# Attention values with the softmax weights stationary: three narrow matmuls per query block and key tile

## The chip, the cores and the metric

The kernel runs on one core of a Trainium2 chip. The metric is the time of one execution in device microseconds, as the median of several runs. The core has a matrix engine (TensorE, PE in the profile, its weight loads PEld), VectorE (DVE), ScalarE (ACT), GpSimd (POOL) and the queue of SyncE (SP), which here issues nearly all DMAs. Matmul results land in PSUM, eight banks of 512 f32 columns in each of 128 partitions.

## What is computed

The program is a layer of a perceiver: cross attention of 512 latent rows on 8192 context rows, then a state-space block, a gated MLP and a mixture of experts. The change lies in the attention:

```
q = (scale * (Q @ Wq + bq)).reshape(bs, q_len, NH, DM)      # 512 rows, NH = 16 heads, DM = 64
k = (K @ Wk + bk).reshape(bs, kv_len, NH, DM)               # 8192 rows
v = (V @ Wv + bv).reshape(bs, kv_len, NH, DM)
qk = jnp.einsum('nlhd,nshd->nhls', q, k)
a = jax.nn.softmax(qk, axis=-1)
o = jnp.einsum('nhls,nshd->nlhd', a, v).reshape(bs, q_len, NH * DM)
return o @ Wo + bo
```

## The kernel before

Products are made from f16 pairs: a number is split into a high part and a low part, and high x high, high x low and low x high are added in PSUM, without low x low.

`context_keys_values` projects the context in 16 chunks of 512 rows, splits keys and values, and stores them in HBM as `kd` and `vd`. In the values tile `vs` each head and key tile has 128 columns: 64 of the high part, 64 of the low part.

`attention` then runs head by head. A key tile has 128 keys, a pair is two of them, so a head has HP = 32 pairs and the stage 512. For a pair:

- TensorE makes the scores transposed, keys on partitions and the 512 queries in columns, with four matmuls of 512 columns (L938, L939) into one of three PSUM buffers `st`.
- ScalarE takes the exponent into `pf`, f32, 128 x 1024 (L771). The high part `ph` is a copy in f16, made by ScalarE for even pairs (L765) and by VectorE for odd ones (L814). VectorE subtracts for the low part `pl` (L818). `pf` has 4 buffers, `ph` and `pl` have 8.
- TensorE adds the values into `acc` (`values`, L890). The value tile is stationary and the softmax weights move, 512 queries wide: for `ph` one matmul per key tile with all 128 columns of `vs` (L900), for `pl` two with 32 columns of the high part each, placed on column groups of the array so that four run at once (L907), and the sum of the weights over the keys by 32 columns of ones, again four at a time (L915). This goes in groups of SP = 4 pairs: the scores of four pairs, then the values of the four pairs before (LAG = 1 group).

At a head's end VectorE copies both banks of `acc` into `parts` (L824, L825). SP stores the sums to HBM and moves the high and low halves onto the partitions of their head in a pair of heads (`store`). For each two heads the sums are read back spread over 128 partitions (`factors`), VectorE adds them and takes the reciprocal (`reciprocals`), SP sends it through HBM so that each partition gets all 512, VectorE scales (`scale`), and ScalarE and VectorE write the split result `oh`, `ol` (`high`, `low`). In the stage's tail TensorE projects with Wo, pair of heads by pair of heads (L957 to L965), VectorE reads the result (L860) and normalizes the rows, and TensorE transposes them (L971).

The order of the work is written out: `turns` and `pair_turns` unroll the steps of one head or two, and the end of a head comes on VectorE two pairs after the head's last pair (`HP + 2`).

Of the kernel before, what the change touches and what calls it, by code (L numbers as in the profile page):

```python
# [21 lines left out]
P = 128  # L22
T = 512
# [67 lines left out]
WT = TW * (NCK // 2 - 1)  # L91

# [166 lines left out]
def context_keys_values(nc, keep, ctxT, q_dram, kd, vd, m_dram, mrow, m_out, wpack, wsplit):  # L259
# [6 lines left out]
    with ExitStack() as ctx:  # L266
# [4 lines left out]
        vs = [m.sb(f"vs{i}", [P, NH, CK // P, 2 * DH], F16) for i in range(2)]  # L271
# [11 lines left out]
        made = m.sem("made")  # L283
# [33 lines left out]
        def _(sp):  # L317
# [12 lines left out]
            def chunk(g, par, i, tiles, more):  # L330
# [6 lines left out]
                at = g * CK if isinstance(g, int) else i * (2 * CK) + (2 - par) * CK  # L337

                for js in (range(0, 6), range(6, 8)) if isinstance(g, int) and g == NCK - 1 else (range(0, 8),):
# [4 lines left out]
                    sp.dma_start(vd.rearrange("h p s -> p h s")[:, :, bass.ds(at + kts.start * P, len(js) // 2 * P)],  # L344
# [9 lines left out]
            for e in range(TW):  # L354
                load_weights(0, e)
            chunk(0, 0, None, (), True)
# [14 lines left out]
        def _(pool):  # L371
            def chunk(g, par, uses, i, tiles):
                nxt = 1 - par
                for n in range(8):
# [11 lines left out]
                    nc.gpsimd.tensor_tensor(vs[par][:, hs, kt, DH:2 * DH],  # L386
# [8 lines left out]

            identity(nc, pool, ident, made)
# [156 lines left out]
SUMS_AT, SCALE_AT, HIGH_AT, LOW_AT, CUT = 8, 14, 16, 18, 20  # L553
EPS1, EPS2 = 1e-5, 1e-6
LAG = 1

HP = KT // 2
SP = 4
HS = HP // SP

# [11 lines left out]
def attention(nc, keep, x, q_dram, m_dram, mrow, m_out, kd, vd, sums, r_dram, bv, bo, n1w, wsplit, xs_dram):  # L572
# [3 lines left out]
    with ExitStack() as ctx:  # L576
# [4 lines left out]
        vs = m.sb("vs", [P, KT, P], F16)  # L581
        ones = m.sb("ones", [P, 32], F16)
        pf = m.sb("pf", [P, FULL, 2, T])
        ph, pl = (m.sb(n, [P, RING, 2, T], F16) for n in ("ph", "pl"))
        parts = m.sb("parts", [P, 2, T])
# [4 lines left out]
        both = [m.sb(n, [P, 2, TT]) for n in ("both_var", "both_sd", "both_rs", "both_tmp")]  # L590
        oh, ol = (keep.big[0][:, i * 2 * WC:(i + 1) * 2 * WC].rearrange("p (j t) -> p j t", t=T) for i in range(2))
        a0, a1, rb, bob = (keep.big[1][:, i * 2 * T:(i + 1) * 2 * T].bitcast(F32) for i in range(4))
        dn = keep.big[1][:, 8 * T:8 * T + 64].bitcast(F32).rearrange("p (n c) -> p n c", c=8)
# [4 lines left out]
        acc = m.ps("acc", [P, 2, T])  # L598
        yp = [st[:, t // 2, t % 2, :] for t in range(TT)]
        hT = [st[:, 2, 0, :], st[:, 2, 1, :], acc[:, 0, :], acc[:, 1, :]]  # L600
# [6 lines left out]
        pl_ready, pv_done, acc_read, o_out = (m.sem(n) for n in ("pl_ready", "pv_done", "acc_read", "o_out"))  # L607
        dn_in, r_ready, r_out, rb_in = m.sem("dn_in"), m.sem("r_ready"), m.sem("r_out"), m.sem("rb_in")
        own_dve, consts, vec_in, small_in = m.sem("own_dve"), m.sem("consts"), m.sem("vec_in"), m.sem("small_in")
        s_ready, oh_ready, ol_ready, y_ready = m.sem("s_ready"), m.sem("oh_ready"), m.sem("ol_ready"), m.sem("y_ready")  # L610
# [10 lines left out]

        FK = SP * 2 * P

# [7 lines left out]
        def _(sp):  # L631
# [7 lines left out]
            def load_values(n, q):  # L639
                sp.dma_start(vs[:, q * 2 * QP:(q + 1) * 2 * QP, :].rearrange("p k c -> p (k c)"),  # L640
                             vd.rearrange("h p s -> p h s")[:, bass.ds(n, 1), q * QK:(q + 1) * QK]
                             .rearrange("p h s -> p (h s)")).then_inc(v_in[q], 16)
# [14 lines left out]
            sp.dma_start(bob, bo.partition_broadcast(P)).then_inc(small_in, 16)  # L657
# [4 lines left out]
            def load_next(h):  # L662
# [5 lines left out]

            def store(j, e):

                h = 2 * j + e
                sp.wait_ge(acc_read, 2 * h + 4)
                sp.dma_start(sums[:, bass.ds(h * T, T)],
                             parts[0:P:32, 1, :]).then_inc(o_out, 16)
                for n, a in enumerate((a0, a1)):
                    sp.dma_start(a[e * DH:(e + 1) * DH, :], parts[n * DH:(n + 1) * DH, 0, :]).then_inc(o_out, 16)

            def factors(j):


                sp.wait_ge(o_out, j * 96 + 144)
# [39 lines left out]
        def turns(eng, step, steps, cut, end=None):  # L721


            for s in range(cut):
                step(0, s)
# [1652 lines left out]
```

## Time and profile before

| | us |
|---|---|
| median of 3 runs | 2517.41 |
| lowest and highest run | 2515.1, 2518.72 |
| span of the profiled execution | 2515.4 |
| TensorE busy | 2395.6 |
| VectorE busy | 1974.4 |
| ScalarE busy | 1603.1 |
| GpSimd busy | 672.5 |

The page gives the span of the profiled execution, from the first to the last instruction; what lies around it is not recorded there. Busy time is the time in which at least one instruction of an engine was running. For TensorE the ends of matmuls are modelled (a 512-column f16 matmul is shown with 0.38 us though the next starts earlier), so the pace of matmuls is read from one start to the next. By stage: projection of keys and values up to 863.8 us, attention from 868.4 to 1789.0 us, its projection and norm to 1822.4 us, then the rest.

### The profile page before, as it was taken

How to read it: one execution, taken by the hardware profiler on the slowest of the kernel's cores; microseconds unless marked ns; L12 is line 12 of the kernel's file. 1: busy time of each engine (PE TensorE's matmuls, PEld its weight loads, DVE VectorE, ACT ScalarE, POOL GpSimd, SP SyncE). 2: the span in 40 equal slices, each digit the busy share in tenths (PEclk: the TensorE clock that was granted, in tenths of full speed). 3: DMA queues.
4: the chain of work that ended last, by engine and by line, in shares of the span. 5: the costliest groups of instructions: out<-in, count | busy, mean ns of one | idle time of the engine just before them, and what ended most of it. 6: DMA issues, size and time to landing. Idle time of an engine off the chain costs nothing. (4 is left out here: it accounts for less than half of the span.)

```text
span 2515.4 us, 39361 instructions
## 1 busy us (share of the span) xinstructions
PE 2395.6 (95%) x14111; PEld 1015.0 (40%) x14111; DVE 1974.4 (78%) x1972; ACT 1603.1 (64%) x1974; POOL 672.5 (27%) x461
## 2 busy tenths in 40 slices
PE   7999999999999799999999999999887878999999
PEld 3333333333333244444444444444332333444554
DVE  5777777777777788888888898888679994267996
ACT  5555555565555478777788777888375442137994
POOL 1455555555555400000000000000019990010001
PEclk9999999999999899999999999999999899999999
DMA  7245654455445593433433333333231005139994
GB/s 251 84 151 163 204 167 150 153 173 175 150 133 150 139 267 89 113 102 95 108 88 105 96 100 92 104 94 107 93 138 52 0 0 201 56 146 346 405 405 174
DMA packets 178205, 366.02 MB, mean 146 GB/s; under 512 B 19545, under 2 KB 90329, under 8 KB 174425
## 3 DMA queue, kind: packets, MB, share of 16 engines
q1 hardware_dynamic: 176610, 360.81, 45.1%
q0 software_dynamic: 1280, 4.20, 0.5%
q8 instruction: 38, 0.62, 0.1%
q14 instruction: 29, 0.24, 0.0%
q10 hardware_dynamic: 248, 0.15, 0.0%
HBM read 254.24 MB, written 106.68 MB: 143 GB/s over the span
## 5 line engine op out<-in xcount | busy, mean ns | idle before, releaser
L466 DVE TENSOR_REDUCE kv_mx<-kv_s 128x1024 f32 (+1 forms) x512 | 595.6, 1218 | 222.5 <-PE kv_s L502 222.5
L818 DVE TENSOR_TENSOR at_pl<-at_pf,at_ph 128x1024 f16<-128x1024 f32 x512 | 613.2, 1223 | 113.2 <-ACT at_ph L765 104.4
L771 ACT ACTIVATE at_pf<-at_st 128x1024 f32<-128x1024 f32 x512 | 497.3, 1025 | 187.2 <-PE at_st L939 182.2
L938 PE MATMUL at_st<-keep_big,at_k_cur 128*128 (+1 forms) x1024 | 390.5, 381 | 10.0 <-DMA keep_big<-q_dram 7.1
L939 PE MATMUL at_st<-keep_big,at_k_one 128*128 (+1 forms) x1024 | 388.9, 380 | 0.0
L765 ACT ACTIVATE at_ph<-at_pf 128x1024 f16<-128x1024 f32 x256 | 272.9, 1066 | 0.0
L1135 POOL MEMSET mamba_zero<- 128x2 f32 x1 | 0.1, 100 | 939.8 <-POOLq L60 939.8
L900 PE MATMUL at_acc<-at_ph,at_vs 128*128 128x512 f16 x1024 | 242.4, 379 | 2.9 <-DVE at_pl L818 2.8
L382 POOL TENSOR_TENSOR kv_ksl<-kv_kf,kv_ksh 128x512 f16<-128x512 f32 x128 | 148.0, 1156 | 246.4 <-ACT kv_ksh L410 246.4
L1049 PE MATMUL kv_kp<-first_ch,first_wkh 128*128 128x512 f16 x512 | 195.0, 381 | 4.2 <-DVEq L448 4.2
L407 ACT ACTIVATE kv_kf<-kv_kp,first_bks 128x512 f32<-128x512 f32 x128 | 87.4, 683 | 169.7 <-PE kv_kp L1049 169.7
L1049 PE MATMUL kv_kp<-first_ch,first_wkl 128*128 128x512 f16 x512 | 195.1, 381 | 0.0
L1049 PE MATMUL kv_vp<-first_wvh,first_ch 128*128 128x512 f16 x512 | 194.5, 380 | 0.3 <-DVE kv_mx L466 0.3
L1049 PE MATMUL kv_kp<-first_cl,first_wkh 128*128 128x512 f16 x512 | 194.8, 380 | 0.0
L1049 PE MATMUL kv_vp<-first_wvl,first_ch 128*128 128x512 f16 x512 | 194.6, 380 | 0.0
L1049 PE MATMUL kv_vp<-first_wvh,first_cl 128*128 128x512 f16 x512 | 194.2, 379 | 0.0
L414 ACT ACTIVATE kv_vf<-kv_vp 128x512 f32<-128x512 f32 x128 | 76.1, 594 | 184.6 <-PE kv_vp L1049 184.6
L386 POOL TENSOR_TENSOR kv_vs<-kv_vf,kv_vs 128x512 f16<-128x512 f32 x128 | 148.0, 1156 | 129.7 <-ACT kv_vs L416 129.7
L1516 PE MATMUL ms_yp<-ms_hc,keep_ident 128*128 128x512 f32 x256 | 133.6, 664 | 46.1 <-POOL ms_hc L1380 33.7
L814 DVE CAST at_ph<-at_pf 128x1024 f16<-128x1024 f32 x256 | 177.3, 693 | 0.0
L938 PEld LDWEIGHTS at_st<-keep_big,at_k_cur 128*128 128x128 f16 x1024 | 100.2, 98 | 171.7 <-issue 54.6
L1392 POOL TENSOR_TENSOR ms_b<-mamba_u,keep_big 128x1024 f32<-128x1024 f32 x63 | 146.5, 2353 | 55.8 <-DVE ms_b L1448 55.3
(351 smaller groups left out, 3859.7 us busy)
## 6 DMA issues: line engine op xcount, KB each, us to landing
keep_big<-gate_up SPq DMA_DIRECT2D x17, 2048.0 KB, 13.1
at_vs<-vd SPq DMA_DIRECT2D x64, 512.0 KB, 3.9
at_k_cur<-kd SPq DMA_DIRECT2D x126, 256.0 KB, 3.8
vd<-kv_vs SPq DMA_DIRECT2D x15, 2048.0 KB, 7.7
kv_tf<-wpack SPq DMA_DIRECT2D x21, 1024.0 KB, 6.4
keep_big<-down SPq DMA_DIRECT2D x17, 1024.0 KB, 13.2
first_cf<-ctxT SPq DMA_DIRECT2D x16, 1024.0 KB, 12.9
ex_yg<-gate_up SPq DMA_DIRECT2D x8, 2048.0 KB, 13.4
```

What stands on the lines that cost most here:

```text
L382: nc.gpsimd.tensor_tensor(ksl[par][:, n, :], kf[:, n % 4, :], ksh[par][:, n, :], ALU.subtract).then_inc(kl_ready, 1)
L386: nc.gpsimd.tensor_tensor(vs[par][:, hs, kt, DH:2 * DH], vf[:, n % 4, :].rearrange("p (h d) -> p h d", d=DH), vs[par][:, hs, kt, 0:DH], AL ...
L466: nc.vector.reduce_max(mx[:, bass.ds(g * (NH * TT) + 2 * (m - TT), 2)], s1[:, m % 3, :, :], AX.X).then_inc(s1_max, 1)
L765: nc.scalar.activation(ph[:, s % RING, :, :], pf[:, s % FULL, :, :], ACT.Copy).then_inc(ph_ready, 1)
L771: nc.scalar.activation(pf[:, s % FULL, :, :], st[:, s % HP % NST, :, :], ACT.Exp, scale=SCORE).then_inc(pf_ready, 1)
L814: nc.vector.tensor_copy(ph[:, s % RING, :, :], pf[:, s % FULL, :, :]).then_inc(ph_own, 1)
L818: nc.vector.tensor_tensor(pl[:, s % RING, :, :], pf[:, s % FULL, :, :], ph[:, s % RING, :, :], ALU.subtract).then_inc(pl_ready, 1)
L900: nc.tensor.matmul(acc[:, 0, :], vs[:, 2 * s + e, :], ph[:, s % RING, e, :], start=(s == 0 and e == 0), stop=False)
L938: nc.tensor.matmul(st[:, w % NST, e, :], k_cur[:, tile], qh[:, q], start=True, stop=False)
L939: last = nc.tensor.matmul(st[:, w % NST, e, :], k_one[:, tile], ql[:, q], start=False, stop=True)
L1049: last = nc.tensor.matmul(out, a, b, start=(start and n == 0), stop=(stop and n == len(pairs) - 1))
L1392: nc.gpsimd.tensor_tensor(b[i % RB][:, :, :], u[:, :].unsqueeze(1).to_broadcast([P, HN, T]), bb[q], ALU.mult).then_inc(b_ready, 1)
```

## The change

The roles in the value product are swapped. The stationary operand is a block of softmax weights, 128 keys by 128 queries, and the values move. For each key tile e and each of the TT = 4 query blocks t there are three matmuls on one accumulator of 128 queries by 65 columns: `ph` with the high values and a column of ones (65 columns), `ph` with the low values (64), `pl` with the high values and the ones (65). The four accumulators lie in one PSUM bank, 128 columns apart; the first half of a head's pairs goes to one bank, the second to the other.

The values tile gets VW = 130 columns per key tile: 64 high, a one, a zero, 64 low. GpSimd writes the ones and zeros once before the chunks. VectorE copies the first bank in mid-head (`first_half`), adds the second at the end, takes the reciprocal of column 64 and scales (`end`) into `o`, f32, queries on partitions. The sums' way through HBM is gone. After the loop TensorE transposes `o` for each pair of heads (`turn`), ScalarE and VectorE split it, and the projection follows. TensorE's steps are single pairs now, with LAG = 4 pairs; the end of a head comes on VectorE after the fourth pair of the next.

```diff
+VW = 2 * DH + 2
+ONE = DH
...
-        vs = [m.sb(f"vs{i}", [P, NH, CK // P, 2 * DH], F16) for i in range(2)]
+        vs = [m.sb(f"vs{i}", [P, NH, CK // P, VW], F16) for i in range(2)]
...
+            for v in vs:
+                nc.gpsimd.memset(v[:, :, :, ONE:ONE + 1], 1.0).then_inc(unit_ready, 1)
+                nc.gpsimd.memset(v[:, :, :, ONE + 1:ONE + 2], 0.0).then_inc(unit_ready, 1)
...
-LAG = 1
+LAG = 4
...
-SP = 4
-HS = HP // SP
...
+        av, osum, rc = m.sb("av", [P, TT, ONE + 1]), m.sb("osum", [P, TT, ONE + 1]), m.sb("rc", [P, TT])
+        o = keep.big[1].bitcast(F32).rearrange("p (t n) -> p t n", t=TT)
+        part_acc = [acc[:, b, :].rearrange("p (t c) -> p t c", t=TT)[:, :, 0:ONE + 1] for b in range(2)]
...
+            def first_half(h):
+                dve.wait_ge(pv_done, h * HP + HP // 2 + RING)
+                nc.vector.tensor_copy(av[:, :, :], part_acc[0]).then_inc(acc_read, 1)
+
             def end(h):
                 dve.wait_ge(pv_done, h * HP + HP + RING)
-                dve.wait_ge(o_out, h * 48 + 48)
-                nc.vector.tensor_copy(parts[:, 0, :], acc[:, 0, :]).then_inc(acc_read, 1)
-                nc.vector.tensor_copy(parts[:, 1, :], acc[:, 1, :]).then_inc(acc_read, 1)
...
+                dve.wait_ge(acc_read, h * 2 + 3)
+                nc.vector.tensor_tensor(osum[:, :, :], av[:, :, :], part_acc[1], ALU.add).then_inc(acc_read, 1)
+                dve.wait_ge(acc_read, h * 2 + 4)
+                nc.vector.reciprocal(rc[:, :], osum[:, :, ONE]).then_inc(sum_ready, 1)
+                dve.wait_ge(sum_ready, h + 1)
+                nc.vector.tensor_tensor(o[:, :, bass.ds(h * DH, DH)], osum[:, :, 0:DH],
+                                        rc[:, :].unsqueeze(2).to_broadcast([P, TT, DH]), ALU.mult).then_inc(o_ready, 1)
...
+            def values(h, s):
+
+
+                if s % QP == 0:
+                    pe.wait_ge(v_in[s // QP], 16 * (h + 1))
+                pe.wait_ge(pl_ready, h * HP + s + 1 + RING)
+                part, at = divmod(s, HP // 2)
+                if at == 0:
+                    pe.wait_ge(acc_read, h * 2 + 1 + part)
+                for e in range(2):
+                    for t in range(TT):
+                        tok, to = slice(t * P, (t + 1) * P), part_acc[part][:, t, :]
+                        v = vs[:, 2 * s + e, :]
+                        nc.tensor.matmul(to, ph[:, s % RING, e, tok], v[:, 0:ONE + 1], start=(at == 0 and e == 0 and t == 0),
+                                         stop=False, skip_group_check=True)
+                        nc.tensor.matmul(to[:, 0:DH], ph[:, s % RING, e, tok], v[:, ONE + 2:VW], start=False, stop=False,
+                                         skip_group_check=True)
+                        last = nc.tensor.matmul(to, pl[:, s % RING, e, tok], v[:, 0:ONE + 1], start=False,
+                                                stop=(at == HP // 2 - 1 and e == 1), skip_group_check=True)
+                last.then_inc(pv_done, 1)
...
             def step(h, d):
 
-                ahead, w = divmod(d, HS)
-                for s in range(SP * w, SP * (w + 1)):
-                    scores(h, ahead, s)
+                ahead, w = divmod(d, HP)
+                scores(h, ahead, w)
                 if d >= LAG:
                     values(h, d - LAG)
...
+            def turn(j):
+
+                pe.wait_ge(o_ready, 2 * j + 2)
+                if j >= 2:
+                    pe.wait_ge(ol_ready, j - 1)
+                for t in range(TT):
+                    last = nc.tensor.transpose(oT[j % 2][:, t * P:(t + 1) * P], o[:, t, j * P:(j + 1) * P], ident[:, :])
+                last.then_inc(oT_ready, 1)
...
+            turn(0)
+            turn(1)
+            for s in range(HP - LAG, HP):
+                values(NH - 1, s)
...
+            for j in range(LATE):
+                project(j, range(TT))
+                turn(j + 2)
+            for t in range(TT):
+                for j in range(LATE, PAIRS):
+                    project(j, (t,))
```

On TensorE, in the loop of the attention, the kernel before has the scores of four pairs and then the values of four (here the last scores of a group, then its value part; `at_st` holds the scores, `keep_big` the queries, register instructions set addresses and waits):

```order
L938 MATMUL at_st<-keep_big,at_k_cur 128x512
L939 MATMUL at_st<-keep_big,at_k_one 128x512
L896 REGISTER_ALU
L900 MATMUL at_acc<-at_ph,at_vs 128x512 x2
L896 REGISTER_ALU
L900 MATMUL at_acc<-at_ph,at_vs 128x512 x2
L896 REGISTER_ALU
L900 MATMUL at_acc<-at_ph,at_vs 128x512 x2
L896 REGISTER_ALU
L900 MATMUL at_acc<-at_ph,at_vs 128x512 x2
L907 MATMUL at_acc<-at_pl,at_vs 32x512 x16
L915 MATMUL at_acc<-at_ph,at_ones 32x512 x2
```

L915 comes eight times x2. In the changed kernel one pair's scores stand between the narrow matmuls of two pairs:

```order
L872 REGISTER_ALU
L876 MATMUL at_st<-keep_big,at_k_cur 128x512
L877 MATMUL at_st<-keep_big,at_k_one 128x512
L876 MATMUL at_st<-keep_big,at_k_cur 128x512
L877 MATMUL at_st<-keep_big,at_k_one 128x512
L841 REGISTER_ALU
L849 MATMUL at_acc<-at_vs,at_ph 128x65
L851 MATMUL at_acc<-at_vs,at_ph 128x64
L853 MATMUL at_acc<-at_vs,at_pl 128x65
```

The group of four pairs is gone, and each pair has its three kinds of narrow matmul eight times over.

On VectorE, at the end of a head, the kernel before copies the two banks of `acc` between subtractions (`at_pl`):

```order
L814 CAST at_ph<-at_pf 128x1024
L818 TENSOR_TENSOR at_pl<-at_pf,at_ph 128x1024
L817 REGISTER_ALU
L818 TENSOR_TENSOR at_pl<-at_pf,at_ph 128x1024
L822 REGISTER_ALU
L823 ISA
L824 COPY at_parts<-at_acc 128x512
L825 COPY at_parts<-at_acc 128x512
L812 REGISTER_ALU
L814 CAST at_ph<-at_pf 128x1024
L818 TENSOR_TENSOR at_pl<-at_pf,at_ph 128x1024
```

In the changed kernel three instructions that depend on each other stand there, before the next subtraction:

```order
L767 CAST at_ph<-at_pf 128x1024
L771 TENSOR_TENSOR at_pl<-at_pf,at_ph 128x1024
L779 REGISTER_ALU
L780 ISA
L781 TENSOR_TENSOR at_osum<-at_av,at_acc 128x260
L782 REGISTER_ALU
L783 RECIPROCAL at_rc<-at_osum 128x4
L784 REGISTER_ALU
L785 ISA
L785 TENSOR_TENSOR keep_big<-at_osum,at_rc 128x4x64
L770 REGISTER_ALU
L771 TENSOR_TENSOR at_pl<-at_pf,at_ph 128x1024
```

The small steps for each two heads (L832 to L844) stand in the loop no more; a copy of the first bank (`at_av`) stands in mid-head.

On TensorE, in the projection after the loop, the kernel before has only products:

```order
L1049 MATMUL at_st<-at_k_cur,keep_big 128x512 x2
L1049 MATMUL at_st<-at_k_one,keep_big 128x512
L1049 MATMUL at_st<-at_k_cur,keep_big 128x512 x2
L1049 MATMUL at_st<-at_k_one,keep_big 128x512
L1049 MATMUL at_st<-at_k_cur,keep_big 128x512 x2
```

In the changed kernel four transpositions stand between the products of two pairs of heads:

```order
L1005 MATMUL at_st<-at_k_one,keep_big 128x512
L1005 MATMUL at_st<-at_k_cur,keep_big 128x512
L893 MATMUL at_st<-keep_ident,keep_big 128x128 x4
L1005 MATMUL at_st<-at_k_cur,keep_big 128x512
L1005 MATMUL at_st<-at_k_one,keep_big 128x512
L1005 MATMUL at_st<-at_k_cur,keep_big 128x512 x2
```

This comes six times, and two such groups stand before the last four pairs' values.

## Rows read from the trace of the kernel before

**Rows 1.** Stretch; busy us (count) of PE, PEld, DVE, ACT, POOL; clock, DMA share, GB/s

```profile
868.40:1789.00 920.60, 914.78 (x7168) 386.85 (x7168) 804.39 (x849) 728.49 (x775) 13.73 (x9) 1.00 0.41 110
```

**Rows 2.** Waits in 900 to 1780: engine line, us in total, times, longest

```profile
ACT at_pf L771 <- PE at_st L939: 176.1, 123, 1.5
DVE at_pl L818 <- ACT at_ph L765: 96.3, 94, 3.2
```

**Rows 3.** Order of time, TensorE, one group: start, us, engine, line, count

```profile
1302.47 1.89 PE L900 MATMUL at_acc<-at_ph,at_vs 128*128 128x512 f16 x8
1304.29 1.05 PE L907 MATMUL at_acc<-at_pl,at_vs 128*32 128x512 f16 x16
1305.17 0.38 PE L915 MATMUL at_acc<-at_ph,at_ones 128*32 128x512 f16 x2
...
1306.14 0.39 PE L938 MATMUL at_st<-keep_big,at_k_cur 128*128 x1
```

**Rows 4.** Order of time, VectorE, the same group

```profile
1303.08 1.22 DVE L818 TENSOR_TENSOR at_pl<-at_pf,at_ph 128x1024 f16<-128x1024 f32 x1 [1.04 <-ACT at_ph L765]
1304.22 0.69 DVE L814 CAST at_ph<-at_pf 128x1024 f16<-128x1024 f32 x1
1304.94 2.36 DVE L818 TENSOR_TENSOR at_pl<-at_pf,at_ph 128x1024 f16<-128x1024 f32 x2
1307.22 0.69 DVE L814 CAST at_ph<-at_pf 128x1024 f16<-128x1024 f32 x1
```

**Rows 5.** Order of time, ScalarE, the same group

```profile
1300.16 1.94 ACT L771 ACTIVATE at_pf<-at_st 128x1024 f32<-128x1024 f32 x2 [1.47 <-PE at_st L939]
1301.99 1.06 ACT L765 ACTIVATE at_ph<-at_pf 128x1024 f16<-128x1024 f32 x1
1302.93 1.94 ACT L771 ACTIVATE at_pf<-at_st 128x1024 f32<-128x1024 f32 x2
...
1307.29 1.94 ACT L771 ACTIVATE at_pf<-at_st 128x1024 f32<-128x1024 f32 x2 [1.47 <-PE at_st L939]
```

**Rows 6.** Order of time, VectorE, two heads' ends and the small steps

```profile
993.65 0.68 DVE L824 COPY at_parts<-at_acc 128x512 f32<-128x512 f32 x1
994.25 0.68 DVE L825 COPY at_parts<-at_acc 128x512 f32<-128x512 f32 x1
...
1005.50 0.20 DVE L834 RECIPROCAL keep_big<-keep_big 128x8 f32<-128x8 f32 x1
...
1051.26 0.68 DVE L825 COPY at_parts<-at_acc 128x512 f32<-128x512 f32 x1
```

**Rows 7.** TensorE's narrow matmuls in the expert stage; two stretches as in rows 1

```profile
2239.84 0.82 PE L1049 MATMUL ex_up<-keep_router,keep_hidden 128*128 128x16 f16 x25 [1.72 <-PEq L60]
2245.31 0.32 PE L1049 MATMUL ex_op<-ex_mask,ex_ones 128*128 128x16 f16 x7
2275.84 0.61 PE L2200 MATMUL ex_gp<-ex_ident,ex_xr 128*128 128x128 f16 x8 [0.35 <-issue]
2239.80:2241.20 1.40, 1.36 (x49) 1.40 (x50) 0.00 (x0) 1.39 (x1) 1.39 (x38) 0.50 0.33 35
2245.10:2245.50 0.40, 0.38 (x15) 0.38 (x16) 0.40 (x1) 0.38 (x2) 0.00 (x0) 1.00 1.04 430
2275.80:2276.40 0.60, 0.56 (x8) 0.46 (x8) 0.00 (x0) 0.00 (x0) 0.00 (x0) 1.00 0.81 256
```

**Rows 8.** Order of time, the tail of the attention

```profile
1786.63 0.61 PE L900 MATMUL at_acc<-at_ph,at_vs 128*128 128x512 f16 x2 [1.26 <-DVE at_pl L818]
1789.01 0.39 PE L1049 MATMUL at_st<-at_k_cur,keep_big 128*128 128x512 f16 x1
1804.47 0.75 DVE L844 SCALAR_TENSOR_TENSOR keep_big<-keep_big,at_bvs 128x512 f16<-128x512 f32 x1 [0.79 <-ACT keep_big L778]
1806.22 0.69 DVE L860 SCALAR_TENSOR_TENSOR keep_x<-at_st,at_pf 128x512 f32<-128x512 f32 x1 [0.99 <-PE at_st L1049]
1818.01 1.91 PE L971 MATMUL at_acc<-keep_ident,at_pf 128*128 128x128 f32 x8
```

More of the change, by code:

```diff
@@ L355, in _ @@
                 load_weights(0, e)
+            sp.wait_ge(unit_ready, 4)
             chunk(0, 0, None, (), True)
@@ L569, in act_highs, with attention @@
     return n // 8 * (8 - len(DVE_HI)) + sum(k not in DVE_HI for k in range(n % 8))
-def attention(nc, keep, x, q_dram, m_dram, mrow, m_out, kd, vd, sums, r_dram, bv, bo, n1w, wsplit, xs_dram):
+def attention(nc, keep, x, q_dram, m_dram, mrow, m_out, kd, vd, bv, bo, n1w, wsplit, xs_dram):
     with ExitStack() as ctx:
@@ L712, in _ @@
             own = Chain(pool, const_ready)
-            own.done(nc.gpsimd.memset(ones[:, :], 1.0))
             for first, end in zip(CONST_PAIRS, CONST_PAIRS[1:] + (HP,)):
@@ L784, in _ @@
             act.dma_start(ql[DH:DH + 1, 0:T], mrow[0:TT, :]).then_inc(q_in, 16)
-            pair_turns(act, pair, lambda h: None, {HIGH_AT: high}, lambda: act.wait_ge(consts, 2))
-            high(PAIRS - 1)
+            turns(act, pair, CUT)
+            act.wait_ge(consts, 2)
+            for j in range(PAIRS):
+                act.wait_ge(oT_ready, j + 1)
+                nc.scalar.activation(oh[:, j, :], oT[j % 2], ACT.Identity, bias=bvs[:, j:j + 1]).then_inc(oh_ready, 1)
             act.wait_ge(var_ready, 1)
@@ L842, in low @@
             def low(j):
                 dve.wait_ge(oh_ready, j + 1)
-                nc.vector.scalar_tensor_tensor(ol[:, bass.ds(j, 1), :].rearrange("p o t -> p (o t)"), a0,
-                                               bvs[:, bass.ds(j, 1)], oh[:, bass.ds(j, 1), :].rearrange("p o t -> p (o t)"),
+                nc.vector.scalar_tensor_tensor(ol[:, j, :], oT[j % 2], bvs[:, j:j + 1], oh[:, j, :],
                                                ALU.add, ALU.subtract).then_inc(ol_ready, 1)
-            pair_turns(dve, pair, end, {SUMS_AT: reciprocals, SCALE_AT: scale, LOW_AT: low}, scaled)
@@ L849, in _ @@
-            reciprocals(PAIRS - 1)
+            turns(dve, pair, CUT, (first_half, end), scaled)
+            low(0)
+            low(1)
+            end(NH - 1)
+            for j in range(2, PAIRS - 1):
+                low(j)
             dve.wait_ge(small_in, 32)
             for t in range(TT):
-                nc.vector.tensor_tensor(xs[:, t, :], xs[:, t, :], bob, ALU.add).then_inc(xs_ready, 1)
-            scale(PAIRS - 1)
+                nc.vector.tensor_tensor(xs[:, t, :], xs[:, t, :], bob[:, :], ALU.add).then_inc(xs_ready, 1)
@@ L855, in _ @@
             low(PAIRS - 1)
-            own.n = 4 * PAIRS
             dve.wait_ge(xs_ready, TT)
@@ L2313, in program @@
         keep.router = [m.sb(f"router{i}", [P, DC, NE], F16) for i in range(2)]
-        attention(nc, keep, x, q_dram, m_dram, mrow, m_out, kd, vd, sums, r_dram, bv, bo, n1w, wsplit, xs_dram)
+        attention(nc, keep, x, q_dram, m_dram, mrow, m_out, kd, vd, bv, bo, n1w, wsplit, xs_dram)
         with ExitStack() as inner:
```

170 lines of the change are left out of this document (42 added, 128 removed).

## The prediction

> **What bounds the kernel now.** I read four views in this order: the busy times by stretch, the waits inside the attention stage, the order of time on each engine there, and the few narrow matmuls that the program already has.
>
> Attention takes 920.6 us of the 2515.4, and in it TensorE is busy 914.8 us at a granted clock of 1.00, VectorE 804.4, ScalarE 728.5 [rows 1]. Two waits tell the rest: ScalarE waits for the scores (176.1 us), VectorE for ScalarE (96.3) [rows 2]. Nothing that TensorE waits for is on that list, so it sets the pace. It works in groups of four key-tile pairs: ScalarE starts the same exponent at 1300.16 and again at 1307.29 [rows 5], so a group takes 7.13 us, a pair 1.78, and 512 pairs 912 us. The other 8.6 us of the stage are filling and draining.
>
> In a group the value part runs from 1302.47 to 1306.14, 3.67 us [rows 3]: eight full matmuls of 512 columns (1.89 less the 0.38 of one, over seven intervals: 0.2157 us each), 16 on 32 columns of the array, four at a time, then 16 for the sums, also four at a time. That is 8 + 4 + 4 = 16 times 0.2157 = 3.45, and 0.22 more where the array form changes. The scores are 16 full matmuls, 3.45 us.
>
> VectorE does two pairs in 3.00 us (from one cast at 1304.22 to the next at 1307.22) [rows 4], ScalarE two exponents and a copy in 2.77 (1300.16 to 1302.93) [rows 5]. Per pair: TensorE 1.78, VectorE 1.50, ScalarE 1.39. So VectorE is late next, and at most 0.28 us per pair can be had before it decides.
>
> **The change, part by part.**
> TensorE, values. Per pair the 2 full, 4 quarter-width value and 4 sum matmuls (3.67/4 = 0.92 us) go. In come 24 matmuls with a 128x128 block of softmax weights stationary: 16 of 65 columns, 8 of 64, each with a weight load of its own. No row has a 65-column matmul; two kinds of neighbour do. With 128 moving columns and a load each, eight run in 0.61 us, one lasting 0.219: 0.0559 us each [rows 7]. With 16 moving columns, seven run in 0.32 less 0.169: 0.025 us each at full clock, and 25 in 0.82 less 0.174: 0.027 at half clock [rows 7]. From 128 to 512 columns the price rises by (215.7 - 55.9)/384 = 0.416 ns a column and leaves 2.6 ns over, so there columns are all that is paid, and the load is hidden. At 16 columns that line would give 9 ns; the 25 to 27 measured are a floor for load plus matmul. I take the greater of line and floor: 65 columns 29.7 ns, 64 columns 29.3. Sum: 16 x 29.7 + 8 x 29.3 = 710 ns. The cheap bound is the floor, 24 x 26 = 624 ns. The dear bounds are the straight line from the 16-column to the 128-column row, 39.0 ns each (936 ns), and, if only that more columns never cost less, 55.9 each (1342 ns). I stay at 710 because 65 lies above the point (about 57 columns) where line and floor meet, and because both rows have a fresh 128x128 load before each matmul, as here, and the 16-column ones also accumulate again and again on one address.
>
> The rows show no price for the load beside a matmul of 128 columns. The Trainium skill (TensorE: Matmul & The Clock Gate, Back-to-back issue gap) gives about 81 ns per matmul for a sustained stream of load and matmul at 128 columns; the trace disagrees with its 55.9. With 81 ns as a ceiling for each of the 24 the value part would be 1.94 us and the time about 3050 us. The same page (LDWEIGHTS) gives columns divided by 1.2 in nanoseconds for a load, 107 for 128 columns; as a pace that is against the 25 to 27 per load and matmul here.
>
> TensorE, scores: unchanged, 4 x 0.2157 = 0.863 us. Pair: 0.863 + 0.710 = 1.573 against 1.781. All matmuls of the loop now use the whole array, so the 0.22 us per group goes too; it is in the 0.92 already. 512 x 1.573 = 805 us against 912, **107 us less**. Steps are now single pairs with four pairs between scores and values; before it was one group of four, so filling and draining stay near 8.6 us. The two early transposition groups (1.7 us) lie in the drain, where TensorE waited 1.26 us anyway [rows 8].
>
> VectorE per head. It drops two PSUM copies of 512 columns at 0.60 us spacing [rows 6], and per two heads the reciprocals, sum, scale and low part. It adds a 260-column copy (between 0.30, in proportion to 0.60, and 0.45: I take 0.40), a 260-column add (0.45), a reciprocal of 4 (as the 8-wide one, 0.20, with 0.03 for waiting on the result before it) and a 256-column multiply (0.40): 1.5 us. Head: 16 x 3.00 + 1.5 = 49.5 us, against TensorE's 32 x 1.573 = 50.3. So it is hidden, but by 0.8 us a head only. Behind the three-instruction end (about 1.1 us in one piece) the next subtraction is queued, and behind that the values of that pair on TensorE. The lag covers it nearly: a pair's values start about 6.0 us after its scores are done, and its subtraction is ready at about 5.1 for the odd pair (exponent, ScalarE copy of its even neighbour, subtraction, cast, subtraction), which leaves 0.9. I put the stall at 0.2 us or less per head, inside the rounding of the forecast. The first-half copy has 0.4 us and no such neighbour.
>
> SP and DMA. All stores of parts, sums and reciprocals go; key and value loads keep their places, the values 1.6% larger. They are hidden: in the stage the DMA share is 0.41. ScalarE loses its per-pair-of-heads activation inside the loop. The key/value stage before writes with a stride of 130 in place of 128, and GpSimd sets four small columns first; TensorE decides there and I cost both at nothing (were the cover gone, each under 1 us).
>
> Tail. The projection started at 1789.01, and the first row block was read at 1806.22 [rows 8]. Now TensorE has six more groups of four f32 transpositions between the projections: eight took 1.91 us, less the 0.42 of one over seven is 0.21 each, 0.86 a group, 5.1 in all. The last pair of heads must be turned, read by ScalarE and by VectorE (0.79 and 0.75) [rows 8] before the last product; of those 1.7 us 0.65 lie beside another product, 1.0 stays. The tail grows by **6 us**; the DMA trip that is removed there was hidden behind the projections.
>
> **Sum.** 2515.4 - 107 + 6 = 2414.6 for the profiled execution. Its span lies 2.0 us under the median of the runs, 2517.4. Forecast **2417 us**.
>
> **The rivals.**
> *VectorE decides.* With 49.5 against 50.3 us a head a small excess is enough. If the 1.45 us of extras are not covered in any head, 16 x 1.45 = 23 us come on top: 2440. Against it is the 0.9 us of lag, for it that this lag is shorter than the 1.1 us piece. The other way, if TensorE were at its floor, VectorE alone would set 16 x 49.5 = 792 us: about 2403, or 2398 with the extras at 0.3 us each.
> *Loads half hidden (the slower side).* If 65 columns cost the straight line between the two neighbours, 39.0 ns, the pair takes 1.80 us: 512 x 0.226 = 116 us over the forecast, 2533, slower by 0.6%. The point from which it decides is 37.7 ns per narrow matmul: 100 us of gain are 12288 x 8.2 ns. For it: the load must fit beside half the columns of the row that hides it. Against: the 16-column rows show that load and matmul together need only 25 to 27 ns.
> *Loads exposed or instructions too slow.* With 55.9 ns each the pair takes 2.20 us and the time is 2740. The same place is reached if TensorE cannot take instructions fast enough for long: 64 instructions in the quarter-width stretch take 1.85 us (1304.29 to 1306.14) [rows 3], 29 ns each, and 48 at that pace are 1.39 us, time 2764. Against: that stretch is paid by columns, and the 50 instructions of the 16-column stretch ran at 13 ns. But it lasted 1.3 us, not 800. The rule of 81 ns above would belong here, with 3 in 100 of the 9.
>
> **How the numbers follow.** Forecast 60%, VectorE 14%, half hidden 17% (spread from 33 to 45 ns, half of it under 37.7), exposed or slow supply 9%. The forecast's own range is 2403 to 2430. For 8 in 10 I go from 2398 to **2485**, which is 35 ns per narrow matmul (512 x 24 x 5.4 ns = 66 us more) and takes in the VectorE case. 0.2% or 5 us is about what a measurement here can tell from no change. Faster by more: 60 + 14 + 8 = 82%; within: 2%; slower: 16%.
>
> **What would show it.** In the changed profile: narrow matmuls 24 to a pair, starts 29 to 30 ns apart (right), 39 (half hidden), over 50 (exposed). The distance from one head's end on VectorE to the next, 57.01 us now [rows 6], should be 50.3 to 50.6; 49.5 with VectorE never idle means that it decides, over 52 with TensorE waiting for the subtraction means its rival. From the last value matmul to the first row block of the projection read: 17.2 us now, 23 after. Wrong would also be a granted clock under 1.00 in the stage, or a key/value stage that is longer.

## The result, and the profile after

The changed kernel takes 2494.7 us (median of four runs, 2491.11 to 2500.32), the kernel before 2516.95 beside it (2515.1 to 2518.72). The ratio is 0.9915, with a 95% interval from 0.9901 to 0.9929. So it is faster, but by 22 us (under 1%) where 100 were forecast, and the time lies above the range's upper end of 2485. The profiled execution has a span of 2489.4 us, 26.0 less than before.

The page of the changed kernel: busy time and share of each engine with its number of instructions, then, from the list of DMA queues, the one that loads instructions (packets, MB, share of the 16 engines' span).

```profile
PE 2315.0 (93%) x21311; PEld 1211.6 (49%) x21311; DVE 1972.6 (79%) x1956; ACT 1618.3 (65%) x1974; POOL 668.1 (27%) x464
...
q8 instruction: 171, 2.80, 0.5%
```

Before, that queue moved 38 packets. It moves 171 now, of 16 KB each (2.80 MB over 171). The attention from its first scores (869.3) to the start of the projection (1759.0), in the columns of rows 1:

```profile
869.30:1759.00 889.70, 830.93 (x14344) 580.21 (x14345) 800.70 (x833) 740.68 (x770) 12.09 (x9) 0.98 0.40 110
```

Before, TensorE was busy 914.78 of 920.60 us at a clock of 1.00 [rows 1]. Now it has 84 us less work but stands still for 58.8 us. The waits of the changed kernel from 900 to 1760 (columns of rows 2):

```profile
ACT at_pf L726 <- PE at_st L877: 130.4, 257, 7.9
PEld at_st L876 <- issue: 55.5, 23, 7.4
DVE at_pl L771 <- ACT at_ph L720: 54.3, 21, 7.8
PE at_st L876 <- issue: 51.9, 14, 7.3
```

The first and third line answer to rows 2, and both waits have become shorter. The fourth has no counterpart there: 14 times TensorE stood still before the first scores matmul (L876) without any semaphore, buffer or engine that the trace would name, 51.9 us in all, the longest (the first) 7.3, the others 3.1 to 3.7. TensorE's loop over the heads has 15 turns, so it jumps back 14 times. The steady pace, on the other hand, is what was forecast. TensorE of the changed kernel, order of time (start, us, engine, line), one value part and the scores behind it:

```profile
1300.31 0.19 PE L849 MATMUL at_acc<-at_vs,at_ph 128*128 128x65 f16 x1
1300.34 0.20 PE L851 MATMUL at_acc<-at_vs,at_ph 128*128 128x64 f16 x1
1300.38 0.19 PE L853 MATMUL at_acc<-at_vs,at_pl 128*128 128x65 f16 x1
...
1301.04 0.38 PE L876 MATMUL at_st<-keep_big,at_k_cur 128*128 x1
...
1301.90 0.19 PE L849 MATMUL at_acc<-at_vs,at_ph 128*128 128x65 f16 x1
```

The 24 narrow matmuls run from 1300.31 to 1301.04: 0.73 us, 30.4 ns each (forecast 0.710 and 29.6). From value part to value part it is 1.59 us (1300.31 to 1301.90; forecast 1.573). 32 such pairs are 50.9 us, a head's period. The first scores matmuls after a turn of TensorE's loop over the heads start elsewhere, though:

```profile
996.33 0.39 PE L876 MATMUL at_st<-keep_big,at_k_cur 128*128 x1 [3.63 <-issue]
1050.77 0.39 PE L876 MATMUL at_st<-keep_big,at_k_cur 128*128 x1 [3.41 <-issue]
1105.44 0.39 PE L876 MATMUL at_st<-keep_big,at_k_cur 128*128 x1 [3.64 <-issue]
```

A head takes 54.4 and 54.7 us, 50.9 and 3.5 to 3.8 more, nearly all of it the stop. TensorE around the third of them, us by us: stretch, its length, busy us (count), granted clock, share of the DMA engines, GB/s.

```profile
1101.00:1102.00 1.00, 0.80 (x25) 1.00 0.00 0
1102.00:1103.00 1.00, 0.00 (x0) 1.00 0.22 46
1103.00:1104.00 1.00, 0.00 (x0) 1.00 0.74 146
1104.00:1105.00 1.00, 0.00 (x0) 1.00 0.86 345
1105.00:1106.00 1.00, 0.56 (x3) 1.00 0.09 29
```

While TensorE stands still the DMA engines, idle just before, become busy. In 1100 to 1600, some nine turns, the instruction queue moves 82 packets in the changed kernel, nine a turn, and none in the kernel before:

```profile
q8 instruction: 82, 1.34, 1.1%
```

The loop of the kernel before has 953 TensorE instructions in a turn, that of the changed kernel 1849 (counted in the built program, a matmul and its weight load as two). That is the suspicion that the experiments had to test: the longer body is no longer held where TensorE takes its instructions from, and each jump back to its beginning has to wait until they are loaded anew.

### The profile page after: what moved, and what is told of

It reads as the page before. It is cut to its first block and busy times, and to the rows that moved or that the text cites. A ratio compares the mean times of both kernels' runs of the same rounds, so it can differ in the third digit from the quotient of the medians.

```text
span 2489.4 us, 53654 instructions
## 1 busy us (share of the span) xinstructions
PE 2315.0 (93%) x21311; PEld 1211.6 (49%) x21311; DVE 1972.6 (79%) x1956; ACT 1618.3 (65%) x1974; POOL 668.1 (27%) x464
## 5 line engine op out<-in xcount | busy, mean ns | idle before, releaser
L771 DVE TENSOR_TENSOR at_pl<-at_pf,at_ph 128x1024 f16<-128x1024 f32 x512 | 624.0, 1225 | 86.6 <-ACT at_ph L720 60.6
L726 ACT ACTIVATE at_pf<-at_st 128x1024 f32<-128x1024 f32 x512 | 522.0, 1020 | 147.3 <-PE at_st L877 138.2
L876 PE MATMUL at_st<-keep_big,at_k_cur 128*128 (+1 forms) x1024 | 393.1, 384 | 61.0 <-issue 51.9
L849 PE MATMUL at_acc<-at_vs,at_ph 128*128 128x65 f16 x4096 | 428.4, 193 | 2.7 <-DVE at_pl L771 2.6
L851 PE MATMUL at_acc<-at_vs,at_ph 128*128 128x64 f16 x4096 | 428.5, 194 | 2.1 <-issue 2.1
L853 PE MATMUL at_acc<-at_vs,at_pl 128*128 128x65 f16 x4096 | 426.5, 192 | 0.1
L849 PEld LDWEIGHTS at_acc<-at_vs,at_ph 128*128 128x128 f16 x4096 | 379.6, 97 | 65.1 <-DVE at_pl L771 4.3
L851 PEld LDWEIGHTS at_acc<-at_vs,at_ph 128*128 128x128 f16 x4096 | 377.8, 97 | 60.6 <-issue 1.9
L853 PEld LDWEIGHTS at_acc<-at_vs,at_pl 128*128 128x128 f16 x4096 | 378.3, 99 | 2.6 <-issue 2.5
```

Source lines behind the costliest of these rows:

```text
L726: nc.scalar.activation(pf[:, s % FULL, :, :], st[:, s % HP % NST, :, :], ACT.Exp, scale=SCORE).then_inc(pf_ready, 1)
L771: nc.vector.tensor_tensor(pl[:, s % RING, :, :], pf[:, s % FULL, :, :], ph[:, s % RING, :, :], ALU.subtract).then_inc(pl_ready, 1)
L849: nc.tensor.matmul(to, ph[:, s % RING, e, tok], v[:, 0:ONE + 1], start=(at == 0 and e == 0 and t == 0), stop=False, skip_group_check=True)
L851: nc.tensor.matmul(to[:, 0:DH], ph[:, s % RING, e, tok], v[:, ONE + 2:VW], start=False, stop=False, skip_group_check=True)
L853: last = nc.tensor.matmul(to, pl[:, s % RING, e, tok], v[:, 0:ONE + 1], start=False, stop=(at == HP // 2 - 1 and e == 1), skip_group_check ...
L876: nc.tensor.matmul(st[:, w % NST, e, :], k_cur[:, tile], qh[:, q], start=True, stop=False)
```

## The experiments

Three explanations stood at the start. **The jump:** the body is fetched again at each turn, at some 3.6 us a time; without a jump the fetching runs ahead and costs nothing. **The head:** something in the order of work at a head's end stops TensorE, whoever writes the loop. **The supply:** TensorE gets through more instructions than can be delivered, and straight code, of which every instruction must be fetched, would be worse.

### TensorE's heads written out, and three heads to a turn

`after_flat` writes out TensorE's loop over the heads; nothing else changes:

```diff
-            turns(pe, step, LAG)
+            for s in range(LAG):
+                step(0, s)
+            for e in range(NH - 1):
+                for s in range(LAG, HP + LAG):
+                    step(e, s)
+            for s in range(LAG, HP):
+                step(NH - 1, s)
```

> The changed kernel with TensorE's attention loop written out in full: no loop, no jump back, the same matmuls in the same order. Theory J (the 3.6 us stall before the first scores of each turn is the jump back to a loop body of 1849 instructions, which is fetched anew each time): no such stall, 15 x 3.6 = 54 us gone, about 2437 us (ratio to the kernel before 0.968). Rival H (the stall belongs to the end of a head: key or value loads, VectorE's three steps): it stays once a head, about 2495 us. Rival S (instructions arrive too slowly for narrow matmuls): more instructions are fetched than before, so it is no better and probably slower than 2495.

Measured: 2428.24 us (2426.22 to 2429.62), 0.964 of the kernel before [0.9624, 0.9656], 66 us below the changed kernel. Its waits from 900 to 1720:

```profile
ACT at_pf L726 <- PE at_st L877: 77.8, 251, 1.2
...
PEld at_acc L849 <- DVE at_pl L771: 7.4, 17, 1.3
DVE at_pl L771 <- ACT at_ph L720: 4.6, 4, 1.4
PE at_acc L849 <- DVE at_pl L771: 2.0, 3, 1.0
```

The stops before the scores are gone, with the same matmuls in the same order. The instructions still have to be fetched; in 1100 to 1600 the instruction queue of this kernel moves:

```profile
q8 instruction: 69, 1.13, 1.0%
```

The head and the supply fall with this run; the jump stays. It gave 2437, 9 us too much: it priced 15 stops at 3.6 us and nothing else, and the section on why the prediction was wrong finds 12.6 us more in the clock.

`after_three` puts three heads into a turn (5537 instructions, 5 turns, so 4 jumps back):

```diff
-            turns(pe, step, LAG)
+            PER = 3
...
+            with pe.Fori(0, (NH - 1) // PER) as j:
+                for e in range(PER):
+                    for s in range(LAG, HP + LAG):
+                        step(j * PER + e, s)
```

> The changed kernel with three heads to a turn of TensorE's loop: 5 turns of 5537 instructions. Theory J: 5 stalls in place of 15, 36 us less, about 2459 us (0.977). Rival H: 15 stalls, 2495. Rival S: no better than 2495.

Measured: 2455.47 us (2451.75 to 2457.2), 0.9746 [0.9729, 0.9762]. The time goes up with the number of jumps, though not in proportion: 0, 4 and 14 of them give 2428, 2455 and 2495. TensorE's waits of this kernel from 869 to 1780:

```profile
PE at_st L876 <- issue: 14.4, 5, 3.8
```

Four of the five are the jumps, 3.3 to 3.8 us each (before the scores at 1044.70, 1200.84, 1359.93 and 1518.17); the fifth is 0.2 us. The row from 869.3 to 1724, by when TensorE has done as many matmuls as `after_flat` by 1696.89, in the columns of rows 1:

```profile
869.30:1724.00 854.70, 831.00 (x14347) 579.41 (x14348) 796.65 (x834) 740.54 (x770) 12.43 (x9) 0.98 0.42 114
```

TensorE is idle 23.7 us there and busy 831.0, against 9.2 and 818.4 of `after_flat` (row in the next section): 14.5 us of standing and 12.6 of a lower clock make up the 27 us between the two kernels. The clock is why the price is not in proportion. It falls to 0.50 after three of these four stops, and also after two stops of 3.2 and 2.7 us within the first head and within the second (at 898.56 and 939.06), where there is no jump. Those two are put down to "issue" as well and come while the DMA engines are full; `after_flat` has such stops too, of up to 1.3 us.

### The kernel before, with a longer turn

If the length of the body is the cause, the old kernel must catch it too. `before_two` and `before_three` give it two heads a turn (1901 instructions, 7 turns, 6 jumps back) and three (2849, 5 turns, 4 jumps), with the edit above in the terms of the old loop (HS for HP).

> The kernel before with two heads to a turn of TensorE's loop (7 turns of 1901 instructions, about as many as in the changed kernel's turn of 1849; before 953), wide matmuls as before. Theory J: 7 stalls of 3.6 us where there were none, some 20 to 25 us slower, about 2540 us (1.009). Rivals H and S: no stall, 2517.

> The kernel before with three heads to a turn: 5 turns of 2849 instructions. Theory J: 5 stalls of 3.6 us, 14 to 18 us slower, about 2533 us (1.006), so less than with two heads to a turn although the body is larger. Rivals H and S: 2517.

Measured: 2537.12 us (2533.98 to 2541.18), 1.0076 [1.0059, 1.0093], and 2531.72 (2528.52 to 2533.63), 1.005 [1.0033, 1.0066]. Both are slower than the kernel before, by under 1% but clear of the noise, though they jump 6 and 4 times where it jumps 14 times; 19 us for 6 jumps and 14 for 4 are 3.2 and 3.4 us a jump. From 869.3 to 1789, TensorE of `before_two`:

```profile
PE at_st L938 <- issue: 15.2, 6, 3.6
```

and in 1100 to 1600 its instruction queue:

```profile
q8 instruction: 40, 0.66, 0.6%
```

That is one stop for each jump, 2.1 to 3.6 us. So the stop has nothing to do with narrow matmuls or the new accumulators. A body of about 1900 instructions brings it, one of 953 does not.

### Where the limit lies

`less_8` and `less_16` are the changed kernel without the middle matmul (the low part of the values, L851) in 8 and in 16 of a head's 32 pairs. They don't compute that product, so their times are to be read for the stop alone. The edit for 8:

```diff
-                        nc.tensor.matmul(to[:, 0:DH], ph[:, s % RING, e, tok], v[:, ONE + 2:VW], start=False, stop=False,
-                                         skip_group_check=True)
+                        if s % 4:
+                            nc.tensor.matmul(to[:, 0:DH], ph[:, s % RING, e, tok], v[:, ONE + 2:VW], start=False,
+                                             stop=False, skip_group_check=True)
```

> The changed kernel without the matmul of the low values in 8 of the 32 pairs (its work is left out): a turn of 1721 instructions. To find the size from which a turn is fetched anew. Theory J: either no fetch at all in the stage after the first turn, or 7 to 8 pages of 16 KB a turn and the stall of 3.6 us; I expect the fetches still there (1901 and 1849 are fetched).

> The changed kernel without the matmul of the low values in 16 of the 32 pairs (its work is left out): a turn of 1593 instructions. Theory J: if a turn of this size is held, no fetches and no stall, and the time falls by 54 us plus up to 40 for the work; if not, 7 pages a turn and the stall. I expect it held, with 55% confidence.

Measured, in a single execution each: 2470.25 us with 1721 instructions in a turn, 2407.73 with 1593. TensorE's waits of `less_8` from 869.3 to 1789, then its instruction queue in 1100 to 1600:

```profile
PE at_st L877 <- issue: 52.6, 14, 8.3
...
q8 instruction: 85, 1.39, 1.2%
```

With 1593 instructions the same queue moves nothing in that stretch and the stop is gone; TensorE's longest list entry, 960 to 1640, is another one:

```profile
PEld at_acc L849 <- DVE at_pl L771: 103.6, 234, 1.0
```

Here TensorE, with less to do, waits for VectorE's subtraction 234 times in some 13 heads, so VectorE decides. The first saves 24 us for 8 pairs of missing work, the second 63 more for 8 others: the difference is the stops, less what VectorE now holds back. The limit in this program lies between 1593 and 1721 instructions. Whether the body's place in its 16 KB pages shifts it was not tried. The Trainium skill (Runtime: NRT & Kernel Launch, Instruction fetch mechanics) describes the mechanism: instructions come in blocks of 16 KiB, or 256 of them, TensorE holds 128 KiB or 2048 of them, and a taken branch whose target lies outside the current window of two such pages has to wait for a fetch. The packets' size, the stop and its place at the jump agree. The two sizes do not: with a window of two pages, 512 instructions, the jumps over 953, 1336 and 1593 instructions would have to fetch, and they don't; and 2048 is too large as a limit, since here 1721 are loaded anew at each turn.

### Two narrow matmuls where there were three

`merged` keeps the change's idea, but multiplies the high part of the weights with high and low values at once, in one matmul of 130 columns, so that a turn has 1336 instructions. The two halves lie side by side in an accumulator over both banks, and VectorE copies and adds them at the head's end.

```diff
-                        nc.tensor.matmul(to, ph[:, s % RING, e, tok], v[:, 0:ONE + 1], start=(at == 0 and e == 0 and t == 0),
+                        nc.tensor.matmul(to, ph[:, s % RING, e, tok], v[:, 0:VW], start=(s == 0 and e == 0 and t % 2 == 0),
                                          stop=False, skip_group_check=True)
-                        nc.tensor.matmul(to[:, 0:DH], ph[:, s % RING, e, tok], v[:, ONE + 2:VW], start=False, stop=False,
-                                         skip_group_check=True)
-                        last = nc.tensor.matmul(to, pl[:, s % RING, e, tok], v[:, 0:ONE + 1], start=False,
+                        last = nc.tensor.matmul(to[:, 0:ONE + 1], pl[:, s % RING, e, tok], v[:, 0:ONE + 1], start=False,
```

> All the work is done, in a smaller loop: the two matmuls with the high softmax weights become one of 130 columns (high values, one, zero, low values), so a pair has 16 narrow matmuls and the turn 1336 instructions in place of 1849. Both banks are then in use by one head, so VectorE copies both (0.6 us) before the next head's values may start. Theory J with the loop held on the core at this size: no stall at the turn and no instruction fetches in the stage; pair 0.863 + 8 x 0.057 + 8 x 0.030 = 1.56 us, about 2425 us (0.963), perhaps 0.5 us a head more for the exposed copy (2433). Rival H (the stall is at the head's end): 2485. If the size that is held is under 1336: 2480.

> The same merged matmuls with TensorE's loop written out in full. Theory J: the loop of the run beside it costs nothing, so the two agree within 0.3%, this one at best 5 us slower from instruction fetches behind the busy queues of the stage's first 60 us. If it is more than 10 us faster, the merged loop still pays for its jumps.

Measured: 2438.9 us (2435.61 to 2441.51), 0.9681 [0.9665, 0.9697], and, with TensorE's heads written out as well, 2439.57 (2435.5 to 2440.32), 0.9684 [0.9668, 0.9701]. The loop costs nothing when its body is held: the two are the same, where for the body of 1849 instructions they lay 66 us apart. Steady values of `merged`, order of time:

```profile
1301.82 0.22 PE L841 MATMUL at_acc<-at_vs,at_ph 128*128 128x130 f16 x1
1301.88 0.19 PE L843 MATMUL at_acc<-at_vs,at_pl 128*128 128x65 f16 x1
1301.91 0.22 PE L841 MATMUL at_acc<-at_vs,at_ph 128*128 128x130 f16 x1
...
1302.52 0.38 PE L866 MATMUL at_st<-keep_big,at_k_cur 128*128 x1
```

Eight such couples take 0.70 us (1301.82 to 1302.52), so a pair is 1.56. But the time is 6 to 14 us over what was expected. The waits from 960 to 1660:

```profile
PEld at_acc L841 <- DVE at_pl L767: 25.1, 26, 1.7
...
PE at_acc L841 <- DVE at_pl L767: 16.2, 13, 1.3
DVE at_av L772 <- PE at_acc L843: 7.1, 14, 0.5
```

Once a head, VectorE waits 0.5 us for the last value matmul, and then TensorE 1.2 us for the subtraction queued behind the head's end: this is the prediction's rival "VectorE decides", in the version whose end is longer.

### What is left, and the best version

Three edits against that wait, and against the first stretch of the stage, in which the DMA engines are full (share 1.03 to 1.05 from 868 to 930 in the kernel before, the changed one and `after_flat`): LAG 5 for 4, so that values run one pair later; END_AT 1 for 0, so that VectorE ends a head one pair later; and the zero write to xs_dram, on SP ahead of the loop of key and value loads, moved behind it:

```diff
             sp.dma_start(bob[:, :], bo.partition_broadcast(P)).then_inc(small_in, 16)
-            sp.wait_ge(none_ready, 1)
-            sp.dma_start(xs_dram.rearrange("(s p) n -> p s n", p=P),
-                         none[:, :].unsqueeze(1).to_broadcast([P, SLOTS, 2 * D])).then_inc(none_out, 16)
...
                     load_values(h + 1, q)
+            sp.wait_ge(none_ready, 1)
+            sp.dma_start(xs_dram.rearrange("(s p) n -> p s n", p=P),
+                         none[:, :].unsqueeze(1).to_broadcast([P, SLOTS, 2 * D])).then_inc(none_out, 16)
```

> The changed kernel with TensorE's loop written out (2428 us), and the 5.9 MB write of zeros to xs_dram issued by SP after the loop of the heads in place of before it. In the stage's first 60 us TensorE stands still for about 5 us more than later, while the DMA engines are full (share 1.03). Theory: instruction pages wait in those queues, so with the write gone the first 60 us have 3 to 5 us less idle time, 2424 us (0.9625). Rival: the idle time there is the first keys' loading or the filling of the pipeline, no change, 2428 (0.964).

> TensorE's loop written out, and five pairs in place of four between a pair's scores and its values. If VectorE's piece at the head's end is not covered by the lag of four, a longer lag gives back the 7 us in which TensorE's value part waited for the subtraction: 2421 us (0.9615). If TensorE's own pace of 1.59 us a pair is all, 2428 (0.964).

> The merged matmuls of 130 columns in the loop of 1336 instructions (2439 us), with a lag of five pairs and the head's end one pair later on VectorE. There TensorE waited 25 us for subtractions and VectorE 7 us for the head's last values. If those waits are the jitter of two engines with equal load, a longer lag takes most of them: 2418 to 2425 us (0.962). If VectorE's own load (49.9 us a head) decides, at most 5 us: 2435.

> The run beside it with the write of zeros after the heads' loop. Its loop fetches no instructions after the first turn; the first turn's pages still come in the stage's first 60 us. As for the written-out loop: 3 to 5 us less if pages wait behind that write, else no change against the run beside it.

With three matmuls neither edit does anything: `flat_late` 2428.28 us (2427.49 to 2429.77), 0.9646 [0.9629, 0.9662], `flat_lag5` 2429.11 (2426.83 to 2430.44), 0.9648 [0.9632, 0.9664]. TensorE decides there, and 2 us of waiting for the subtraction are all there is to win. With two matmuls the lag and the later end count (both are changed in this run, and which of them does it is not shown): `merged_lag5` takes 2418.04 us (2415.37 to 2420.02), 0.9602 [0.9586, 0.9618], 21 less than `merged`, and its wait for the subtraction is gone. What it waits for in the first stretch, 872 to 960, is a load:

```profile
PEld at_st L866 <- issue: 7.9, 6, 5.9
PE at_st L866 <- DMA at_k_one<-kd: 5.7, 1, 5.7
```

These are the second head's keys, issued right behind the zero write (5.9 MB, landed after 25.5 us). With the write moved, `merged_lag5_late` takes 2411.36 us (2410.46 to 2412.47), 0.9577 [0.9561, 0.9593]; the wait is gone, and from 868 to 930 TensorE gets more done. First line `merged_lag5`, second `merged_lag5_late`, in the columns of rows 1:

```profile
868.00:930.00 62.00, 51.48 (x581) 33.58 (x582) 52.28 (x51) 48.34 (x50) 17.01 (x12) 0.91 1.03 275
...
868.00:930.00 62.00, 58.01 (x664) 37.48 (x664) 54.97 (x55) 54.42 (x57) 14.39 (x11) 0.94 0.97 215
```

This version does all the work and is the fastest of them: 107 us below the kernel before, run beside it (2518.02), and 83 below the changed one. ScalarE's wait for scores, 130.4 us in the changed kernel (900 to 1760) and 51.8 in `merged` (960 to 1660), is 29.1 us in 960 to 1640. In those 680 us TensorE is busy 679.7, VectorE 666.3 and ScalarE 627.5, so TensorE sets the pace and the three are close together.

## Why the prediction was wrong

**What failed** is the first step of the part on the change, where the values' cost was worked out as matmuls times duration and nothing else. The step has 24 matmuls a pair in place of 10 and their weight loads; what it leaves out is that they stand in a loop body, written out over a whole head, whose length they take from 953 to 1849 instructions. In the forecast's sum the loop's ends stand at nothing: only "filling and draining stay near 8.6" is added to the pairs. Measured, TensorE stood still 51.9 us at the 14 jumps and lost 12.6 us more to a lower clock. The question "does this loop still fit?" was not asked. The rival "instructions too slow" did name the supply, and weighed it as nanoseconds for each instruction; that was the wrong place. Straight code, fetched all along, runs at 30 ns a matmul (`after_flat`), so supply as a pace is no limit here. The price is per jump, and the prediction had none for it.

**The sum, with what was measured.** The forecast for the profiled execution was 2414.6 (its terms as written, 2515.4 - 107 + 6, give 2414.4), its span is 2489.4, 75 more. From the changed kernel to `after_flat` 61.5 go by taking away the jump alone (span 2427.9); the stage's own rows say how. From 869.3 to the stage's end at 1696.89 in `after_flat`:

```profile
869.30:1696.89 827.59, 818.37 (x14344) 572.17 (x14345) 794.56 (x834) 740.39 (x771) 15.61 (x10) 1.00 0.43 118
```

TensorE is idle 9.2 us here and 58.8 in the changed kernel, 49.6 less: the stops of 51.9, less the 2.0 us by which the first scores start later here (871.34). The rest is in the busy column, 818.4 against 830.9 for the same matmuls: 12.6 us from the clock. Together that is 62 us, the distance between the two stages' ends. The clock falls after some of the stops. The changed kernel at another turn (stretch, length, busy, granted clock, DMA share, GB/s):

```profile
1376.00:1377.00 1.00, 0.00 (x0) 0.89 0.72 200
1377.00:1378.00 1.00, 0.00 (x0) 0.50 0.73 291
1378.00:1379.00 1.00, 0.53 (x2) 0.50 0.08 25
...
1383.00:1384.00 1.00, 1.00 (x22) 0.70 0.00 0
1384.00:1385.00 1.00, 1.00 (x15) 1.00 0.00 0
```

The granted clock falls to 0.50, the 1.2 GHz level, during the stop, and the first 5 us of the next head run at it (3 to 5 us at the five such places). That is so at 5 of the 14 stops (the clock falls at 936, 1376, 1434, 1544 and 1602); at the others, as at 1102 to 1105 above, it stays at 1.00. Why at these five is open: the stops there last 7.3, 3.7, 3.1, 3.6 and 3.1 us, those without it 3.1 to 3.7. The prediction had a clock under 1.00 on its list of signs that it is wrong.

**The other 13 us** are in `after_flat` as well (2427.9 against 2414.6). The stage begins 2.9 us later (first scores at 871.34, 868.40 before) and lasts 825.6 us where 813.6 were forecast, 12.0 more. Of these 10 are the narrow matmul, mis-sized by 0.8 ns (30.4 for 29.6, 12288 times). The other 2 fall in the first 60 us by elimination, where the DMA engines are full and the clock is at 0.95; no run separates them. From the start of the projection to the end of the span it is 731.0 us, 4.6 more than before and not 6, which gives 1.4 back.

**Tail: half right.** From the start of the projection to its first row block it was 17.21 us [rows 8]. The changed kernel:

```profile
1759.02 0.38 PE L1005 MATMUL at_st<-at_k_cur,keep_big 128*128 128x512 f16 x1
...
1761.61 0.60 PE L893 MATMUL at_st<-keep_ident,keep_big 128*128 128x128 f32 x4
1762.05 0.38 PE L1005 MATMUL at_st<-at_k_cur,keep_big 128*128 128x512 f16 x1
...
1779.88 0.69 DVE L806 SCALAR_TENSOR_TENSOR keep_x<-at_st,at_pf 128x512 f32<-128x512 f32 x1 [0.99 <-PE at_st L1005]
```

20.86 us, 3.65 more and not 6. The direction held; the term of the transpositions was mis-sized, 0.44 us a group (1761.61 to 1762.05) where the row at 1818.01 [rows 8] gave 0.86. Six groups at 0.44 and the forecast 1.0 for the last pair make 3.6. The old row stands in a stretch of the kernel before that ran at half clock, behind an idle time of TensorE:

```profile
1818.00:1819.00 1.00, 1.00 (x6) 0.50 0.00 0
```

The prediction took its duration for work that runs at full clock, without the clock beside it.

**Right were** the price of 65 columns next to a fresh load (30.4 ns, far from the 39 and 55.9 of the rivals); the pair (1.59 for 1.573), with TensorE setting it; the extras of VectorE, each within 0.05 us:

```profile
1300.56 0.42 DVE L776 COPY at_av<-at_acc 128x260 f32<-128x260 f32 x1
...
1759.45 0.42 DVE L781 TENSOR_TENSOR at_osum<-at_av,at_acc 128x260 f32<-128x260 f32 x1
1759.90 0.18 DVE L783 RECIPROCAL at_rc<-at_osum 128x4 f32<-128x4 f32 x1
1760.12 0.43 DVE L785 TENSOR_TENSOR keep_big<-at_osum,at_rc 128x256 f32<-128x256 f32 x1
```

and that its stall is small: in `after_flat` TensorE waits 2.0 us for the subtraction from 900 on, 0.13 a head where "0.2 or less" stood. The Trainium skill (TensorE: Matmul & The Clock Gate, Back-to-back issue gap) has 81 ns for a stream of load and matmul at 128 columns; here such a stream at 65 columns runs at 30.4. Loads, stores and the key/value stage cost little (first scores at 869.3 in the changed kernel, 871.3 in `after_flat`, 868.4 before). The head's period was given as 50.3 to 50.6 us; from one head's end on VectorE to the next it is 50.9 without the stop (`after_flat`), 54.4 to 54.7 with it, and 55.6 to 57.2 where the clock fell.

## What to carry to other kernels

Before matmuls are split into more and narrower ones, count the instructions that one turn of the engine's loop then has, weight loads included, beside the counts of loops in the same program that run without stops; if the number grows past them, write the loop out or merge matmuls again. In a profile the sign is an idle time put down to "issue" at the first matmul of each turn, with packets of the instruction queue beside it. And a change whose steady pace was forecast to 1% can still lose three quarters of its gain at a place that occurs 14 times, so price the loop's ends as well as its middle.

## What the runs showed of the hardware

- A loop body of 953, 1336 or 1593 TensorE instructions runs from turn to turn with no packet of the instruction queue (1100 to 1600); one of 1721, 1849 or 1901 is loaded again at each turn, some nine packets of 16 KB (the shortest that is, 8% longer than the longest that isn't). TensorE of the changed kernel then stops 3.1 to 3.7 us (7.3 the first time, when the DMA share was mostly 0.97 to 1.08), that of `before_two` 2.1 to 3.6. Straight code of the same matmuls, all of it fetched (69 packets in 1100 to 1600), runs without a stop once the first 60 us of the stage are over.
- In the changed kernel a stop of under 4 us was followed 4 times in 13 by 3 to 5 us of work at the lower clock (0.50), and at the others by none; in `after_three` 3 times in 4.
- A weight load of 128x128 and a matmul of 65 columns take 30.4 ns together, over 12288 of them; with 130 columns a couple of 130 and 65 takes 88 ns. Four 128x128 f32 transpositions take 0.44 us at full clock.
